# Four row scatters moved to the end of POOL's step in a routed vision tower, one core

## The reference

```
h = patches @ W_tok.T + b_tok                                  # 2048 x 192
n = layernorm(h);  q, k, v = split(n @ W_attn + b_attn)        # 12 heads of 16, rotary on q and k
h = h + softmax(causal(q @ k.T / 4)) @ v @ W_proj + b_proj
n = layernorm(h);  t = rmsnorm(n) * norm_scale
top_vals, top_idx = top_k(t @ gate_w.T + gate_b, 4);  w = softmax(top_vals)
y_e = swiglu(t @ w1[e] + b1[e]) @ w2[e] + b2[e]
out = h + n + sum over the chosen e of w_e * y_e
```

## Time and profile before

| | us |
|---|---|
| median of 3 runs | 570.34 (570.23 to 570.76) |
| the profiled execution | 570.69 |
| its span | 568.7 |
| PE busy | 495.1 |
| DVE busy | 355.5 |
| POOL busy | 253.6 |
| ACT busy | 223.7 |

### The profile page before, as it was taken

The page is one execution under the profiler, slowest core; times in us unless marked ns, Lnnn a source line. Parts: engine busy times, 40 slices in busy tenths (PEclk is TensorE's granted clock), DMA queues, the critical chain, the costliest instruction groups (busy, mean ns, idle before and its releaser), DMA issues.

```text
span 568.7 us, 12728 instructions
## 1 busy us (share of the span) xinstructions
PE 495.1 (87%) x2837; PEld 368.4 (65%) x2838; DVE 355.5 (63%) x1043; ACT 223.7 (39%) x674; POOL 253.6 (45%) x303
## 2 busy tenths in 40 slices
PE   3888879887879741999999999999999999999990
PEld 3666767766756521677777777777777777777760
DVE  1367888788787661556566665656566666656560
ACT  1267766666586311232323323232323233232320
POOL 2114667777766673133343434333343434333342
PEclk9799998999896555899999999999999999999996
DMA  8955564564411135233333332333333332323221
GB/s 231 248 149 157 152 194 146 151 204 149 144 37 47 53 114 162 43 45 49 57 51 51 44 58 44 58 44 54 48 52 50 51 51 44 58 44 57 39 22 21
DMA packets 39744, 49.39 MB, mean 87 GB/s; under 512 B 5355, under 2 KB 30075, under 8 KB 39716
## 3 DMA queue, kind: packets, MB, share of 16 engines
q1 hardware_dynamic: 24308, 33.48, 22.0%
q0 software_dynamic: 14544, 14.94, 17.0%
q10 hardware_dynamic: 864, 0.65, 0.3%
HBM read 30.82 MB, written 18.23 MB: 86 GB/s over the span
## 4 chain that ended last, share of the span: by engine, by line
PE 64%; POOL 12%; issue 8%; DVE 5%; ACT 3%; SPq 3%; DMA 2%; POOLq 1%; DVEq 0%; ACTq 0%
PE bank L543 36%; PE bank L559 13%; POOL routed_rows L1071 8%; PE bank L552 5%; PE bank L536 3%; PE bank L386 2%; ACT k_spread L621 1%; POOL rms L1062 1%; POOL rstd L1062 1%; DMA x_sb<-patches 1%; ACT p_spread L603 1%; SPq L292 1%; DMA out_rows<-x_sb,wproj_sb 1%; PE bank L392 1%; PE bank L412 1%
## 5 line engine op out<-in xcount | busy, mean ns | idle before, releaser
L543 PE MATMUL bank<-w_sb,wqkv_sb 96*128 (+1 forms) x632 | 232.4, 489 | 0.6 <-ACT wqkv_sb L603 0.6
L1127 POOL DMA_INDIRECT out_rows<-x_sb,wtok_sb x50 | 77.9, 1559 | 145.7 <-DMA out_rows<-x_sb,wtok_sb 96.5
L543 PEld LDWEIGHTS bank<-w_sb,wqkv_sb 96*128 96x128 f32 (+1 forms) x632 | 112.2, 192 | 44.8 <-issue 2.1
L603 ACT ACTIVATE p_spread<-bank 128x384 f32<-128x384 f32 x79 | 38.8, 491 | 221.3 <-PE bank L552 221.3
L1021 DVE TENSOR_SCALAR v_sb<-bank 128x384 f32<-128x384 f32 x79 | 44.1, 558 | 101.3 <-PE bank L543 101.3
L559 PEld LDWEIGHTS bank<-w_sb,p_spread 128*128 128x128 f32 x474 | 81.2, 189 | 21.8 <-issue 0.9
L559 PE MATMUL bank<-w_sb,p_spread 128*128 x474 | 90.1, 325 | 0.7 <-ACT p_spread L603 0.7
L1071 POOL DMA_INDIRECT routed_rows<-packet,row_i x64 | 63.3, 989 | 23.6 <-issue 22.4
L1018 DVE TENSOR_SCALAR k_spread<-bank 128x384 f32<-128x384 f32 x79 | 44.0, 557 | 28.7 <-PE bank L543 28.7
L1127 POOL DMA_INDIRECT out_rows<-x_sb,wproj_sb x20 | 31.1, 1555 | 51.8 <-DMA out_rows<-x_sb,wproj_sb 27.3
L386 PE MATMUL bank<-wtok_sb,x_sb 128*128 128x192 f32 x192 | 39.9, 365 | 9.7 <-DMA wtok_sb<-w_tok 5.5
(11 more groups left out here) (148 smaller groups left out, 643.0 us busy)
## 6 DMA issues: line engine op xcount, KB each, us to landing
w_sb<-w SPq DMA_DIRECT2D x16, 576.0 KB
x_sb<-patches SPq DMA_DIRECT2D x16, 384.0 KB, 3.4
wtok_sb<-routed_rows SPq DMA_DIRECT2D x50, 106.0 KB, 2.0
w_sb<-w SPq DMA_DIRECT2D x16, 288.0 KB
wproj_sb<-routed_rows SPq DMA_DIRECT2D x20, 106.0 KB, 2.0
out_rows<-h SPq DMA_DIRECT2D x16, 96.0 KB, 1.9
routed_rows<-packet,row_i POOLq DMA_INDIRECT x64, 2.5
routed_rows<-pad_row SPq DMA_DIRECT2D x9, 106.0 KB, 2.4
```

The costliest lines, as they stand in the source:

```text
L543: last = mm(dst[buf % 2][:, 0:INNER], rT[buf % 2][0:k, c, :], w1_sb[0:k, c, bass.ds(expert, 1), a:a + INNER].rearrange("p a f -> p (a f)") ...
L603: return nc.scalar.activation(dst, src, ACT.Copy)
L1127: G.indirect_dma_start(out=out, out_offset=bass.IndirectOffsetOnAxis(ap=rows[b][:, ID_AT:ID_AT + 1].bitcast(U32), axis=0), in_=y_out[b % N ...
```

## The change

Only POOL's step changes. The scatters of stage 6 stand behind the inverse root from `ssq` and the residual sum in every step, where before they did so only in steps without a stage 2.

```
@@ -1094,13 +1094,11 @@
                     inverse_root(tile(4), mv2[:, 1:2], 1.0, "mv2_ready", ve2, "ve2_ready", rstd2, "x2_ready",
                                  "rstd2_ready")
 
-                if tile(6) is not None and tile(2) is not None:
-                    scatter(tile(6), (n - 6) % 2)
                 if tile(4) is not None:
                     inverse_root(tile(4), ssq[:], 1.0 / DIM, "ssq_ready", msq, "msq_ready", rms, "t_row_ready",
                                  "rms_ready")
                     residual(tile(4))
-                if tile(6) is not None and tile(2) is None:
+                if tile(6) is not None:
                     scatter(tile(6), (n - 6) % 2)
 
             pipeline(pool, STAGES, TILES, step, 2)
```

## The result

| | before | after |
|---|---|---|
| median | 570.55 us | 585.37 us |
| runs | 570.23 to 570.81 | 584.09 to 585.62 |
| profiled execution | 570.69 | 585.37 |
| its span | 568.7 | 583.4 |

The change makes the kernel slower: the ratio is 1.0255, with a 95% interval of 1.0238 to 1.0273, 14.8 us in all. The medians of both kernels were taken together here, so that of before differs a little from the one ahead of the prediction. The forecast was 581.5 us, with a range of 578.5 to 587.

The account below looks back on a forecast made before the run. POOL's token-stage queue, with the scatters as largest share, was taken to bound the kernel; +1.1 (step 6), +8.1 (7 to 15), +1.25 (16) and +0.57 (17) made +11.0 us, so 581.5 us, range 578.5 to 587.

Parts of the forecast that it names:

- The ring: p_pair, turn_probs, DVE's queue to norm2, ACT's square, msq, rms, residual, four scatters, next p_pair: 11.75 us a step against 10.85.
- The open price: POOL, start of the first scatter behind the residual sum: taken at 0.29 us, with ends 0.17 and 0.73.
- Steps 6, 16 and 17: Moved token-stage steps outside 7 to 15: +1.1 us for step 6, +1.25 for 16, +0.57 for 17.
- the sum: Token stage, twelve moved steps: +11.0 us in total, of which steps 7 to 15 give 9 x 0.90 = +8.1.
- The cover of TensorE: PE's chain from turn_probs to attn_add: 9.0 us, 10.8 with a low clock, under 11.75, so a low stretch costs nothing.
- rival A: PE's longer idle gap brings enough low-clock stretches to pass 587 us: PE ring 14.8 us, +39, so 610 us; chance 0.07.
- the term that was set to 0: PE in the loop steps: a stretch at the low clock level in a step costs nothing in the new order.
- the sign of being wrong that it had named: DVE: L813 or attn_add waits for L431 in most steps, which would point to rival A.
- B: POOL's ring is under 10.85 us, so the 1.45 us wait is pure gain: 17 us less, 553 us; chance 0.04.
- C: No change: ring within 0.1 us of 10.85, or another engine sets the pace; 570.3 us; chance 0.04.

Follow-up runs that it names:

- split1: Changed kernel with one of the four scatters ahead of msq, the other three behind the residual sum; 573.22 us, ratio 1.0048 to the kernel before.
- after_fill6: Changed kernel with 6 extra matmuls on PE ahead of its wait for the spread probabilities; 582.11 us, against 584.52 us for the changed kernel unaltered.
- split1 with the extra matmuls: split1 with the 6 extra matmuls of after_fill6 on PE, in steps 6 to 15 alone; 566.56 us, ratio 0.9920 to the kernel before.

## Why the prediction was right, and where it was not

**The ring** was right in its course and its size. Measured in the step without a disturbance: p_pair to turn_probs 1.01 us (1.13 in the working), on to msq 3.95 (4.01), to the residual sum 0.80 (0.79), to the first scatter 0.96 (0.59 + 0.29 = 0.88), to the next p_pair 5.01 (4.93). Sum 11.73 against 11.75. Single terms were off by up to 0.12, and that they evened out to 0.02 is luck. norm2 ahead of the rotary products shows that the ring passes where it was said to pass.

**The open price**, the start of the first scatter, was bounded by 0.17 and 0.73 us and taken at 0.29. It was 0.17 us in every loop step (0.17 to 0.19 in all moved ones), though the residual sum before it grew from 0.58 to 0.79: the nearest row by position decided, not the nearest by kind of step. That the start-up lies under the instructions ahead of it, as the working argued, fits this but is not shown by itself. In steps 7 to 15 of split1, where a scatter stands behind rstd2 again, it is 0.66 to 0.74 again.

**Steps 6, 16 and 17**: p_pair of step 7 was to come at 71.24 and came at 71.19. Steps 16 and 17 were to take 11.28 each and took 11.42 and 11.11. Together with the ring this is the +11.0 us of the sum.

**The cover of TensorE** is the step that failed. The working took the one low stretch of the kernel before as the measure, 3.5 us, found that PE's ring then takes 10.8 us, and concluded that a stretch at the low level costs nothing in the new order. That holds for this length, as after_fill6 shows. But in the new order the stretch is another: 9.6 us in step 7 and 6.8 in each of steps 9, 11, 13 and 15, because a gap of 2.4 us or more comes in each of the ring's undisturbed steps (the working had it at some 3 us, and followed what the clock does in it only in rival A). Steps 8, 10, 12 and 14 (8 pays for step 7, with a clock of 0.59) have 13.36 + 12.66 + 12.59 + 12.36 = 50.97 us where four times 11.75 is 47.0, so the term that was set to 0 measured +4.0 us. With it the sum is 11.0 + 4.0 = 15.0 us against 14.8 measured. Filling the gap takes all four back to 11.73 us (11.72 to 11.75). The working also looked at the projection alone as PE's due date; the embedding, for which DVE waits first (L733), came late ahead of the same steps, with waits of 1.86 to 2.61 us. And the sign of being wrong that it had named, attn_add waiting for L431 in most steps, came true: 8 waits, of which the four of 0.47 to 0.99 us ahead of the turn_probs of steps 8, 10, 12 and 14 count; behind the other four, DVE waited 1.7 us or more for p_pair all the same.

Rival A had the mechanism that made up the difference, and the sentence from the Trainium skill, "TensorE: Matmul & The Clock Gate", Part 1, that activity releases the throttle and idle gaps bring it back, went the right way, and the trace agrees: more low stretches than before (0.59 to 0.71 in five of the steps 7 to 15, where the kernel before has 0.84 in two). Its size was far off, since the clock came back in each next step of the loop; the one step that was low throughout, 17, took 11.11 us and cost nothing that can be seen. It stood as a case of its own at 610 us, where it belonged as a term into the forecast. The change came out at 14.8 us where 11.0 were forecast. That the range held was luck: the upper bound of the scatter's start, which did not occur, had made room for more than 5 us.

**Rivals B and C** fell: the kernel became slower, and the steps took 11.1 us and more. B named the right point of decision, a ring of 10.85 us. split1 with the extra matmuls runs at 10.47 us and is indeed on the other side of it, at 566.6 us.

## What to carry to other kernels

When a wait in a pipelined loop is taken away by moving work, walk the ring that the moved work now closes, from the engine's next instruction all the way round; here the wait of 1.45 us went and one of 2.1 us came. Work that fills a hole on its engine should be cut to about the size of the hole, not moved out of it: one or two scatters in it gave steps of 10.5 us, all four 10.85, none 11.73. And the longer ring gave TensorE a longer gap here: look in the windows at what the granted clock does, and price a low stretch in the step that follows it.

## What was not expected of the hardware

Some instructions with two inputs, on POOL and DVE, take longer where they run beside each other, and the change moved where they do. In the changed kernel the residual sum takes 0.79 us in a loop step (0.58 before), and DVE's rotary sum beside it 0.95 (0.55 before):

```profile
126.44 0.79 POOL L1076 TENSOR_TENSOR h<-h,x 128x192 f32 x1
...
126.70 0.95 DVE L767 TENSOR_TENSOR qk<-rope_c,rope_s 128x384 f32<-128x384 f32 x1
```

In return p_pair takes 0.98 us instead of 1.09, and t_row L843 0.40 to 0.42 instead of 0.75, since t_row no longer runs beside the residual sum and p_pair. Where norm2 stands ahead of the rotary products, the two sums of the changed kernel miss each other and take 0.59 and 0.54 to 0.62 us (shown with that experiment), so it is the overlap that goes with the longer times. The Trainium skill, "SBUF — State Buffer", "Who interferes with whom", says that a VectorE instruction with two inputs in SBUF contends with a GpSimd instruction that reads SBUF. The four instructions here have two such inputs each, and the trace agrees. No run here separates the inputs from other things that could make them longer together. On the ring it comes to +0.2 us for the residual sum and -0.1 for p_pair; the first scatter, 1.19 us instead of 1.07, adds another 0.1, and its cause is open.
